# Attention kernel with convolution layout: squared norms from weights times T in PSUM, and a re-ordered head

## The chip, the cores and the metric

The kernel runs on one core of a Trainium2 chip. The metric is the device time of one execution in microseconds (us). TensorE (PE in the profile) multiplies matrices and writes PSUM, VectorE (DVE) and ScalarE (ACT) do elementwise work, GpSimd (POOL) does elementwise work in SBUF, and SyncE (SP) issues the DMAs.

## The reference, cut to what matters

The input x is 16 images of 192 channels by 48 x 48 pixels (n = 2304), float32. Each image is normalised in 32 groups of 6 channels, goes through a channel attention of 8 heads (d = 24), and is added to the input.

```python
xt = _gn(x).reshape(b, c, n).transpose(0, 2, 1)
q, k, v = jnp.split(xt @ w_qkv, 3, axis=-1)        # heads: q, v (b,h,n,d), k (b,h,d,n)
q = q / jnp.maximum(jnp.sqrt(jnp.sum(q * q, axis=-2, keepdims=True)), EPS)
k = k / jnp.maximum(jnp.sqrt(jnp.sum(k * k, axis=-1, keepdims=True)), EPS) * temperature
attn = _softmax(jnp.einsum('bhpn,bhnq->bhpq', k, q))
out = jnp.einsum('bhnp,bhpq->bhnq', v, attn)        # back to (b, n, c)
out = out @ w_out + b_out
return x + out.transpose(0, 2, 1).reshape(b, c, H, W)
```

## The kernel before, in words

**Algebra.** The attention needs only the Gram matrix of the normalised input, G = x x^T (192 x 192 per image). With T = G W the scores are W_q^T T_k, and the squared norms of q and k are the diagonals of W_q^T T_q and W_k^T T_k. The softmax and the two weight matrices fold into one matrix M of 192 x 192 per image, and the output is x + M x_norm + bias. Every float32 factor is split into a high and a low float16 part (names with h and l), and each product is made of three: high x high, low x high, high x low.

**Tiling.** Two images are one pair; there are 8 pairs. A pair lies in three tiles of 128 partitions (t = 0: channels 0 to 127 of the first image, t = 2: of the second, t = 1: channels 128 to 191 of both) by 2304 columns. A *chunk* is one tile by 768 columns; the nine chunks of a pair, CHUNKS[0] to CHUNKS[8], go group by group of columns, in each t = 0, 2, 1. A *slot* is 128 columns of a pair: TensorE transposes its high and low parts into PSUM (`transposes`, L956), ScalarE copies them to SBUF (`to_tok`, L577, a ring of four), and TensorE adds their product to the Gram matrix (`gram`, L981).

**Steps.** The outer loop is step p = -1 to 7. A step has two halves. In the first, A, the 18 slots of pair p+1 run (`transposes` three slots ahead of `gram`), and between them the small work of pair p: `flip`, softmax_in, exp, softmax_out, `attn_values` ("v"), `folded_weights` ("m"). In the second, B, TensorE makes the 18 results of pair p (`result`, five or so products of 384 columns each, into a ring of four PSUM banks, which VectorE empties into x_sb, L855), and between them the small work of pair p+1: `finish_gram`, `gram_weights` ("w0", "w1": T = G W into g_ps banks 0 and 1 for the two images' first 128 channels and s_ps bank 0 for the other 64 of both), "t0" to "t2" (ScalarE takes the high half of T into tq, VectorE the low half), `scores`, `norms`, `spread`. Step -1 has no results, step 7 no slots.

**The order within an engine** is written out by hand: tables PE_A, PE_B, ACT_A, ACT_B, POOL_B, VEC_A, VEC_B say after which slot (A) or result (B) which piece stands, with a FIRST_ set for step -1 and a LAST_ set for step 7's A half and step 6's B half. `hooks` (L335) picks the table. Each engine runs its own list in order and waits on semaphores.

**Splitting a pair.** While pair p's results run, ScalarE normalises the chunks of pair p+2: "x3" writes the float32 value of chunk 3 to the ring xn (three entries, `chunk_value`), "h3" its float16 high part (`chunk_high`), a bare 3 both. GpSimd's `split` subtracts them to get the low part. "x3" waits until GpSimd has read chunk 0 from the ring; "h" of a chunk with t = 0 waits until a third of the last results with that buffer are made. Both need the scale and shift rb, which GpSimd's `group_power` makes from the variance: VectorE's bn_stats ("bn", `piece`) and `channel_stats` ("stats"), TensorE's `group_sums` ("sums"), VectorE's `group_variance` ("var"). Slots 0 to 5 need chunks 0 to 2, slots 6 to 11 chunks 3 to 5, slots 12 to 17 chunks 6 to 8.

**Norms, scores.** `scores` (L1064) makes, for each image and half of the heads, one chain of 6 products of 192 columns (the columns of w_q and w_k beside each other) with the 96 q columns of T as weights, and one chain of 6 products of 96 columns with the k columns: 48 products. VectorE's `norms` multiplies the two diagonal blocks by the identity, sums and clamps them (four instructions, L768 to L771), GpSimd's `norm_power` raises them to -1/2, and `spread` scales the scores. `flip` transposes them for the softmax.

**Head.** Pair 0 is normalised in smaller parts by all three engines (`first_split`, `first_value`, `first_low`, `first_high`). The float16 weights' high parts are made by ScalarE, the low parts by GpSimd (`low_constants`, in SBUF, through xn); TensorE transposes the value weights behind slot 14 (`transpose_wv`), VectorE splits them (`value_weights`). ScalarE's first three values of pair 1 wait for `low_constants`.

Of the kernel before, what the change touches and what calls it, by code (L numbers as in the profile page):

```python
# [101 lines left out]
def preact_attention(nc, x, w_qkv, temperature, w_out, b_out, ident, ident16, groups, headmask, out):  # L102
# [29 lines left out]
    with ExitStack() as ctx:  # L132
# [48 lines left out]
        tq = sb("tq", [P, 3, 2, 2 * C], F16)  # L181
        dg = sb("dg", [HC, 8, HC])
# [33 lines left out]
        qk_ps = s_ps[0:HC, :, 0:2 * C].rearrange("p b (j s c) -> p b j s c", j=2, s=2)  # L216
        kk_ps = g_ps[0:HC, 0, 0:2 * C].rearrange("p (b j c) -> p b j c", b=2, j=2)
# [71 lines left out]
        STAT, GVAR, NORM, DIAG, SOFT, ATTN = 6, 4, 2, 3, 5, 6  # L289
# [231 lines left out]
        def _(act):  # L521
# [729 lines left out]
```

## Time and profile before

| | us |
|---|---|
| median of 3 runs | 374.44 |
| the runs | 373.13, 374.47, 374.44 |
| the profiled execution's own time | 374.76 |
| its span, first to last instruction | 372.8 |
| busy: TensorE / weight loads | 331.2 (89%) / 233.4 (63%) |
| busy: VectorE / ScalarE / GpSimd | 283.2 (76%) / 235.9 (63%) / 150.4 (40%) |
| chain that ended last, shares | PE 64%, ACT 15%, issue 10%, DVE 5%, DMA 2% |

The page divides the span into 40 slices and prints the busy share of each engine and the granted TensorE clock as digits: TensorE is at 9 tenths or more from the eighth slice on but for two near the end, and the clock is below full speed in the sixth to the eighth (47 to 75 us). The rows of the timeline are merged: "x3" is three instructions from the first's start, the time is up to the last's end. Instructions of one engine overlap, so a pitch (start to start) is shorter than a duration. A time in brackets is how long the engine had been idle before, with what ended the wait.

### The profile page before, as it was taken

How to read it: one execution, taken by the hardware profiler on the slowest of the kernel's cores; microseconds unless marked ns; L12 is line 12 of the kernel's file. 1: busy time of each engine (PE TensorE's matmuls, PEld its weight loads, DVE VectorE, ACT ScalarE, POOL GpSimd, SP SyncE). 2: the span in 40 equal slices, each digit the busy share in tenths (PEclk: the TensorE clock that was granted, in tenths of full speed). 3: DMA queues.
4: the chain of work that ended last, by engine and by line, in shares of the span. 5: the costliest groups of instructions: out<-in, count | busy, mean ns of one | idle time of the engine just before them, and what ended most of it. 6: DMA issues, size and time to landing. Idle time of an engine off the chain costs nothing.

```text
span 372.8 us, 9327 instructions
## 1 busy us (share of the span) xinstructions
PE 331.2 (89%) x3724; PEld 233.4 (63%) x3724; DVE 283.2 (76%) x666; ACT 235.9 (63%) x410; POOL 150.4 (40%) x133
## 2 busy tenths in 40 slices
PE   0048856999999999999999999999999999999795
PEld 0036645875778566865777577856686577765452
DVE  4889855887699669986799769966998665359774
ACT  1098489763997299747996399729974699610200
POOL 0079858301970169203950197016920395001000
PEclk9999976899999999999999999999999999999999
DMA  7999900004994279815991499427981563034766
GB/s 235 359 286 246 244 16 3 2 2 139 300 323 132 86 233 326 247 44 137 336 335 44 134 297 338 124 87 226 320 261 45 165 217 88 2 105 150 230 213 192
DMA packets 30826, 67.73 MB, mean 182 GB/s; under 512 B 5504, under 2 KB 12096, under 8 KB 30784
## 3 DMA queue, kind: packets, MB, share of 16 engines
q1 hardware_dynamic: 30544, 66.56, 56.7%
q10 hardware_dynamic: 240, 0.59, 0.6%
q8 instruction: 29, 0.48, 0.5%
q14 instruction: 13, 0.11, 0.1%
HBM read 29.38 MB, written 28.31 MB: 155 GB/s over the span
## 4 chain that ended last, share of the span: by engine, by line
PE 64%; ACT 15%; issue 10%; DVE 5%; DMA 2%; SPq 2%; POOL 1%; ACTq 0%; POOLq 0%
PE u_ps L927 30%; PE g_ps L927 17%; PE s_ps L927 10%; ACT h_sb L543 4%; ACT tok L581 4%; ACT xn L537 3%; PE u_ps L976 2%; DMA wo<-in_L_conv_w_out_dram 2%; PE u_ps L977 2%; ACT h_sb L550 1%; DVE x_sb L855 1%; PE u_ps L979 1%; PE u_ps L978 1%; SPq L354 1%; SPq L359 1%
## 5 line engine op out<-in xcount | busy, mean ns | idle before, releaser
L474 POOL TENSOR_TENSOR l_sb<-xn,h_sb 128x768 f16<-128x768 f32 x63 | 103.8, 1649 | 56.0 <-ACT h_sb L543 55.7
L855 DVE SCALAR_TENSOR_TENSOR x_sb<-u_ps,bias,x_sb 128x384 f32<-128x384 f32 x144 | 85.9, 613 | 24.2 <-PE u_ps L927 24.1
L927 PE MATMUL g_ps<-tok 128*128 128x64 f16 (+1 forms) x864 | 87.1, 241 | 3.4 <-ACT tok L581 2.9
L537 ACT ACTIVATE xn<-x_sb,rb 128x768 f32<-128x768 f32 x63 | 63.6, 1020 | 29.7 <-POOL rb L486 29.7
L581 ACT COPY tok<-u_ps 128x384 f32<-128x384 f32 x144 | 65.0, 485 | 19.8 <-PE u_ps L979 18.6
L927 PEld LDWEIGHTS g_ps<-tok 128*128 128x128 f16 x864 | 57.0, 99 | 28.5 <-ACT tok L581 5.8
L728 DVE BATCH_NORM_STATS2 bnst<-x_sb 128x6 f32<-128x384 f32 x144 | 69.9, 543 | 5.3 <-DMA x_sb<-in_x_dram 5.2
L927 PE MATMUL u_ps<-h_sb,ml 128*128 128x384 f16 (+1 forms) x336 | 73.2, 327 | 0.0
L543 ACT ACTIVATE h_sb<-x_sb,rb 128x768 f16<-128x768 f32 x63 | 64.4, 1022 | 0.0
L976 PE MATMUL u_ps<-id,h_sb 128*128 128x128 f16 x288 | 48.9, 223 | 8.2 <-DVE l_sb L718 7.4
L977 PE MATMUL u_ps<-id,l_sb 128*128 128x128 f16 x288 | 48.9, 223 | 0.0
L927 PE MATMUL u_ps<-h_sb,mh 128*128 128x384 f16 (+1 forms) x192 | 47.2, 326 | 1.5 <-DVE ml L817 1.5
L480 POOL TENSOR_TENSOR grs<-gvar,minus_half 128x3 f32<-128x3 f32 x8 | 7.1, 885 | 102.6 <-DVE gvar L761 102.6
L927 PE MATMUL u_ps<-hl,mh 128*128 128x384 f16 (+1 forms) x192 | 47.9, 334 | 0.0
L927 PE MATMUL u_ps<-l_sb,mh 128*128 128x384 f16 (+1 forms) x192 | 47.1, 326 | 0.0
L927 PEld LDWEIGHTS u_ps<-h_sb,ml 128*128 128x128 f16 (+1 forms) x336 | 28.9, 101 | 23.9 <-issue 7.3
L976 PEld LDWEIGHTS u_ps<-id,h_sb 128*128 128x128 f16 x288 | 27.4, 100 | 8.6 <-ACT h_sb L550 6.5
L978 PE MATMUL u_ps<-id,h_sb 128*128 128x128 f16 x144 | 32.1, 223 | 0.0
L979 PE MATMUL u_ps<-id,l_sb 128*128 128x128 f16 x144 | 32.1, 223 | 0.0
L977 PEld LDWEIGHTS u_ps<-id,l_sb 128*128 128x128 f16 x288 | 28.8, 100 | 0.4
L927 PEld LDWEIGHTS u_ps<-hl,mh 128*128 128x128 f16 (+1 forms) x192 | 14.7, 103 | 15.0 <-issue 7.5
L491 POOL TENSOR_TENSOR r<-n,minus_half 96x8 f32<-96x8 f32 x8 | 13.3, 1660 | 24.9 <-DVE n L771 24.2
(144 smaller groups left out, 567.6 us busy)
## 6 DMA issues: line engine op xcount, KB each, us to landing
x_sb<-in_x_dram SPq DMA_DIRECT2D x48, 384.0 KB, 5.4
out_dram<-x_sb SPq DMA_DIRECT2D x48, 384.0 KB, 2.9
out_dram<-x_sb SPq DMA_DIRECT2D x48, 192.0 KB, 2.8
x_sb<-in_x_dram SPq DMA_DIRECT2D x45, 192.0 KB, 5.4
hl<-h_sb SPq DMA_DIRECT2D x48, 96.0 KB, 2.8
hl<-l_sb SPq DMA_DIRECT2D x48, 96.0 KB, 3.0
x_sb<-in_x_dram ACTq DMA_DIRECT2D x3, 192.0 KB, 4.2
w<-in_L_conv_w_qkv_dram SPq DMA_DIRECT2D x1, 288.0 KB, 7.4
```

The lines of the kernel that those rows point to most:

```text
L474: nc.gpsimd.tensor_tensor(l_sb[:, par, t, cols], xn[:, c % XN_RING, :], h_sb[:, par, t, cols], ALU.subtract).then_inc(l_ok, 1)
L491: nc.gpsimd.tensor_tensor(r8[:, :], n8[:, :], minus_half[0:HC, :].to_broadcast([HC, 8]), ALU.pow).then_inc(r8_ok, 1)
L537: nc.scalar.activation(xn[:, c % XN_RING, :], xcol(q, t, g * GW, GW), ACT.Identity, bias=rb[:, par, 1, t:t + 1], scale=rb[:, par, 0, t:t + ...
L543: nc.scalar.activation(h_sb[:, par, t, g * GW:g * GW + GW], xcol(q, t, g * GW, GW), ACT.Identity, bias=rb[:, par, 1, t:t + 1], scale=rb[:, ...
L581: nc.scalar.copy(tok[:, j % TOK_RING, :, :].rearrange("p b n -> p (b n)").bitcast(F32), slot_words(j)).then_inc(tok_a, 1)
L728: ins = V.bn_stats(bnst[:, t, 6 * part:6 * part + 6], xcol(q, t, part * BW, BW))
L855: V.scalar_tensor_tensor(out=xs, in0=block_ps(n), scalar=bias[:, t:t + 1], in1=xs, op0=ALU.add, op1=ALU.add).then_inc(out_ok, 1)
L927: return nc.tensor.matmul(dst, lhs, rhs, start=start, stop=stop, skip_group_check=True)
L976: nc.tensor.transpose(bank[:, b, 0:P], h_sb[:, par, 2 * b, px], id16[:, :])
L977: nc.tensor.transpose(bank[:, b, 256:384], l_sb[:, par, 2 * b, px], id16[:, :])
L978: nc.tensor.transpose(bank[:, :, P:P + C1], h_sb[:, par, 1, px], id16[:, :])
L979: nc.tensor.transpose(bank[:, :, P + C1:P + 2 * C1], l_sb[:, par, 1, px], id16[:, :]).then_inc(tr_mm, 1)
```

## The change

1. **Norms.** `scores` keeps only the products of q columns of T with w_k: 24 products of 96 columns. After the low half of T is taken (now only the q half, 192 columns), VectorE multiplies T by the weights elementwise, in place in PSUM. ScalarE ("p", `high_products`) and VectorE ("lo", `low_products`) split the product into float16 parts pw16, and TensorE (`squares`) sums it over the partitions: 24 products with 128 columns of pw16 as weights and a 2-column matrix of ones (`side`) as moving operand. `norms` is left with one clamp.
2. **Tables.** Scores stand after result 10 instead of 12, squares after 12. ScalarE makes x0, x1, x2 ahead of t0, "p" between h1 and h2, and x7 moves from ACT_B to slot 1 of ACT_A; there h8 now stands ahead of exp. GpSimd's norms stand ahead of split 4. The last pair has its own places.
3. **Second pair.** In step 0 flip, v and m stand at slots 5, 12 and 15, and ScalarE's pieces h5 to h8 of pair 1 one behind each slot.
4. **Head.** The value weights are transposed and split before pair 0's first split. The group sums of pair 1 stand behind slot 17, ahead of the Gram matrix's end. VectorE makes the low parts wml (`mixed_weights`) and the first three values of pair 1 (`second_value`), ahead of z.

```diff
-PE_B = {0: ["gram"], 2: ["sums"], 4: ["w0"], 6: ["w1"], 12: ["scores"]}
-ACT_A = {0: ["h6"], 2: ["h7"], 4: ["x8"], 6: ["exp", "h8"], 11: ["v"], 14: ["m"]}
-ACT_B = ["x0", "t0", "t1", "t2", "h0", 1, 2, 3, 4, 5, "x6", "x7"]
-POOL_B = ["power", 0, 1, 2, 3, 4, "norms", 5, 6, 7, 8]
+PE_B = {0: ["gram"], 2: ["sums"], 4: ["w0"], 6: ["w1"], 10: ["scores"], 12: ["squares"]}
+ACT_A = {0: ["h6"], 1: ["x7"], 2: ["h7"], 3: ["x8"], 5: ["h8"], 6: ["exp"], 11: ["v"], 14: ["m"]}
+ACT_B = ["x0", "x1", "x2", "t0", "t1", "t2", "h0", "h1", "p", "h2", 3, 4, 5, "x6"]
+POOL_B = ["power", 0, 1, 2, 3, "norms", 4, 5, 6, 7, 8]
-VEC_B = {0: ["gram"], 2: ["var"], 4: ["z"], 6: ["t0", "t1", "t2"], 12: ["norms"], 17: ["spread", "bn", "bn", "bn", "bn"]}
+VEC_B = {0: ["gram"], 2: ["var"], 4: ["z"], 6: ["t0", "t1", "t2"], 9: ["lo"], 12: ["norms"], 17: ["spread", "bn", "bn", "bn", "bn"]}
-FIRST_PE_A = {14: ["wv"]}
-FIRST_PE_B = {0: ["gram", "sums"], 2: ["w0"], 7: ["w1", "scores"]}
+FIRST_PE_A = {17: ["sums"]}
+FIRST_PE_B = {0: ["gram"], 2: ["w0"], 7: ["w1", "scores", "squares"]}
-FIRST_ACT_B = [0, "x1", "t0", "t1", "t2", "h1", 2, 3, 4, 5, "x6", "x7"]
-FIRST_POOL_B = ["power", 0, 1, 2, 3, 4, "norms", 5, 6, 7, 8]
-FIRST_VEC_A = {17: ["bn"] * 7 + ["stats", "wv"]}
-FIRST_VEC_B = {0: ["gram", "var", "z", "t0", "t1"], 1: ["t2", "bn", "bn", "wo", "norms", "spread", "bn", "bn"]}
+FIRST_ACT_B = ["h0", "h1", "h2", "x3", "t0", "t1", "t2", "h3", "p", "x4", "h4", "x5"]
+FIRST_POOL_B = ["power", 0, 1, 2, 3, 4, 5, "norms", 6, 7, 8]
+FIRST_VEC_A = {17: ["bn"] * 7 + ["stats"]}
+FIRST_VEC_B = {0: ["var", "gram", "wm", "v0", "v1", "v2", "z", "t0", "t1"],
+               1: ["t2", "lo", "bn", "bn", "norms", "wo", "spread", "bn", "bn"]}
+SECOND_PE_A = {5: ["flip"], 12: ["v"], 15: ["m"]}
+SECOND_ACT_A = {0: ["h5"], 1: ["x6"], 2: ["h6"], 3: ["x7"], 4: ["h7"], 5: ["x8"], 6: ["h8"], 8: ["exp"], 14: ["v"], 17: ["m"]}
-LAST_PE_B = {0: ["gram"], 2: ["w0"], 3: ["w1"], 5: ["scores"], 10: ["flip"], 16: ["v"]}
+LAST_PE_B = {0: ["gram"], 2: ["w0"], 3: ["w1"], 6: ["scores"], 7: ["squares"], 11: ["flip"], 16: ["v"]}
-LAST_ACT_B = ["t0", "t1", "t2", "exp", "v"]
+LAST_ACT_B = ["t0", "t1", "t2", "p", "exp", "v"]
-LAST_VEC_B = {0: ["gram"], 2: ["z"], 3: ["t0", "t1", "t2"], 5: ["norms"], 8: ["spread"], 10: ["soft_in"], 12: ["soft_out"],
-              15: ["v"]}
+LAST_VEC_B = {0: ["gram"], 2: ["z"], 3: ["t0", "t1", "t2"], 4: ["lo"], 6: ["norms"], 9: ["spread"], 11: ["soft_in"], 13: ["soft_out"], 15: ["v"]}
...
-                if q == 1 and c < XN_RING:
-
-                    act.wait_ge(low_ok, 8)
...
-                nc.scalar.copy(tq[:, k, 0, :], src[:, 0:2 * C]).then_inc(th_ok, 1)
+                nc.scalar.copy(tq[:, k, 0, :], src[:, 0:C]).then_inc(th_ok, 1)
+
+            def high_products(q):
+
+                need(act, n_mm, q)
+                for k in range(3):
+                    act.wait_ge(pw_ok, 3 * q + k + 1)
+                    nc.scalar.copy(pw16[:, k, 0, 0:2 * C], t_ps(k)).then_inc(ph_ok, 1)
...
+            def mixed_weights():
+
+                dve.wait_ge(high_ok, 1)
+                for b in (0, 1):
+                    r = slice(C1 * b, C1 * b + C1)
+                    V.scalar_tensor_tensor(out=wml[r, b, :], in0=w1[r, qk], scalar=W_SCALE, in1=wmh[r, b, :],
+                                           op0=ALU.mult, op1=ALU.subtract).then_inc(wm_ok, 1)
...
+            def second_value(c):
+
+                t, g = CHUNKS[c]
+                if c == 0:
+
+                    dve.wait_ge(norm, 2 * NORM)
+                    dve.wait_ge(low_ok, 4)
+                V.tensor_scalar(xn[:, c, :], xcol(1, t, g * GW, GW), rb[:, 1, 0, t:t + 1], rb[:, 1, 1, t:t + 1],
+                                ALU.mult, ALU.add).then_inc(xn1_vec, 1)
...
             def norms(q):
 
+                dve.wait_ge(n_mm, q + 1)
+                V.tensor_scalar(n8[:, :], n_ps[0:HC, :], NORM_EPS ** 2 * NORM_FACTOR, None, ALU.max).then_inc(diag, 1)
...
-                V.tensor_tensor(tq[:, k, 1, :], src[:, 0:2 * C], tq[:, k, 0, :], ALU.subtract).then_inc(tl_ok, 1)
+                V.tensor_tensor(tq[:, k, 1, :], src[:, 0:C], tq[:, k, 0, :], ALU.subtract).then_inc(tl_ok, 1)
+                dve.wait_ge(tl_ok, 3 * q + k + 1)
+                V.scalar_tensor_tensor(out=src[:, 0:2 * C], in0=src[:, 0:2 * C], scalar=W_SCALE, in1=(w1 if k == 2 else w0)[:, 0:2 * C],
+                                       op0=ALU.mult, op1=ALU.mult).then_inc(pw_ok, 1)
+
+            def low_products(q):
+                for k in range(3):
+
+                    dve.wait_ge(ph_ok, 3 * q + k + 1)
+                    V.tensor_tensor(pw16[:, k, 1, 0:2 * C], t_ps(k), pw16[:, k, 0, 0:2 * C], ALU.subtract).then_inc(pl_ok, 1)
...
+                        terms = [(tq[:, b, 0, qc], wh0[:, kc]), (tq[:, b, 1, qc], wh0[:, kc]), (tq[:, b, 0, qc], wl0[:, kc]),
+                                 (tq[:, 2, 0, qc], wmh[:, b, kc]), (tq[:, 2, 1, qc], wmh[:, b, kc]),
+                                 (tq[:, 2, 0, qc], wml[:, b, kc])]
+                        for k, (lhs, w) in enumerate(terms):
+                            last = mm(qk_ps[:, b, j, :], lhs, w, k == 0, k == 5)
                 last.then_inc(s_mm, 1)
+
+            def squares(q):
+
+                pe.wait_ge(pl_ok, 3 * q + 3)
+                for a in range(4):
+                    c = C - C * (a // 2) + HC * (a % 2)
+                    terms = [(pw16[:, k, i, c:c + P], side[:, k, :]) for k in range(3) for i in (0, 1)]
+                    dst = n_ps.rearrange("p (s b j) -> p s j b", s=2, b=2)[:, a // 2, a % 2, :]
+                    for k, (lhs, one) in enumerate(terms):
+                        last = mm(dst, lhs, one, k == 0, k == len(terms) - 1)
+                last.then_inc(n_mm, 1)
```

## Rows read from the trace of the kernel before

**Rows 1.** Windows: stretch, length; busy PE, PEld, DVE, ACT, POOL; clock, DMA share, GB/s

```profile
79.80:120.25 40.45, 40.37 (x467) 28.31 (x466) 32.87 (x80) 29.91 (x51) 17.96 (x14) 1.00 0.63 206
```

**Rows 2.** Timeline of TensorE in one pair: start, us, instructions, [idle before]

```profile
124.68 0.32 PE L927 MATMUL u_ps<-parts,grp 128*128 128x6 bf16 x7
124.86 0.32 PE L927 MATMUL u_ps<-h_sb,mh 128*128 128x384 f16 x1
...
136.74 0.33 PE L927 MATMUL s_ps<-wh,tq 128*96 128x192 f16 x2
...
137.23 0.25 PE L927 MATMUL g_ps<-wh,tq 128*96 128x96 f16 x2
...
137.50 0.33 PE L927 MATMUL s_ps<-wh,tq 128*96 128x192 f16 x2
...
139.79 0.33 PE L927 MATMUL u_ps<-h_sb,mh 128*128 128x384 f16 x1
...
153.16 0.25 PE L927 MATMUL s_ps<-wvh,ax 96*96 96x192 f16 x1
```

**Rows 3.** Timeline of ScalarE in the same pair

```profile
127.91 1.03 ACT L537 ACTIVATE xn<-x_sb,rb 128x768 f32<-128x768 f32 x1 [4.43 <-POOL rb L486]
130.96 0.86 ACT L626 CAST tq<-g_ps 128x384 f16<-128x384 f32 x2 [2.02 <-PE g_ps L927]
...
142.23 1.94 ACT L537 ACTIVATE xn<-x_sb,rb 128x768 f32<-128x768 f32 x2
144.62 0.48 ACT L581 COPY tok<-u_ps 128x384 f32<-128x384 f32 x1 [0.46 <-PE u_ps L979]
...
149.98 0.26 ACT L587 ACTIVATE s_ps<-s_ps 96x96 f32<-96x96 f32 x1
...
151.06 1.24 ACT L581 COPY tok<-u_ps 128x384 f32<-128x384 f32 x3
```

**Rows 4.** Timeline of VectorE in the same pair

```profile
131.47 1.02 DVE L848 TENSOR_TENSOR tq<-g_ps,tq 128x384 f16<-128x384 f32 x2 [0.22 <-ACT tq L626]
...
150.27 0.25 DVE L799 TENSOR_REDUCE sm<-s_ps 96x4 f32<-96x96 f32 x1
...
151.06 0.56 DVE L805 TENSOR_TENSOR s_ps<-s_ps,mask 96x384 f32<-96x384 f32 x1
...
152.25 0.55 DVE L808 TENSOR_TENSOR ax<-s_ps,ax 96x384 f16<-96x384 f32 x1
```

**Rows 5.** Timeline of GpSimd in the same pair

```profile
151.26 1.65 POOL L474 TENSOR_TENSOR l_sb<-xn,h_sb 128x768 f16<-128x768 f32 x1 [1.83 <-ACT h_sb L543]
```

**Rows 6.** Chain of work that ended last: start, us, what

```profile
72.21 0.06 PE u_ps L976
...
81.12 0.81 PE u_ps L927 x5
```

**Rows 7.** Timeline of TensorE in the head

```profile
43.90 0.32 PE L927 MATMUL s_ps<-parts,grp 128*128 128x6 bf16 x7
...
80.96 0.33 PE L927 MATMUL u_ps<-h_sb,mh 128*128 128x384 f16 x1
```

**Rows 8.** Timeline of ScalarE in the head

```profile
47.57 1.03 ACT L537 ACTIVATE xn<-x_sb,rb 128x768 f32<-128x768 f32 x1 [3.10 <-POOL rb L486]
...
61.56 0.47 ACT L581 COPY tok<-u_ps 128x384 f32<-128x384 f32 x1
```

**Rows 9.** Timeline of VectorE in the head

```profile
41.69 0.77 DVE L746 CAST parts<-res 128x6 bf16<-128x6 f32 x1
...
53.16 3.23 DVE L689 SCALAR_TENSOR_TENSOR wol<-wo,woh 96x384 f16<-96x384 f32 x2
```

**Rows 10.** Timelines of ScalarE, GpSimd and TensorE for the last pair

```profile
330.08 0.86 ACT L626 CAST tq<-g_ps 128x384 f16<-128x384 f32 x2 [4.37 <-PE g_ps L927]
...
338.15 1.64 POOL L491 TENSOR_TENSOR r<-n,minus_half 96x8 f32<-96x8 f32 x1 [23.46 <-DVE n L771]
...
349.66 0.26 PE L927 MATMUL s_ps<-woh,vh 96*128 96x192 f16 x1 [0.28 <-DVE vl L814]
```

More of the change, by code:

```diff
@@ L180, in preact_attention @@
         z16 = sb("z16", [P, 2, C], F16)
-        tq = sb("tq", [P, 3, 2, 2 * C], F16)
-        dg = sb("dg", [HC, 8, HC])
+        tq = sb("tq", [P, 3, 2, C], F16)
+        pw16 = sb("pw16", [P, 3, 2, 2 * C + P - HC], F16)
+        side = sb("side", [P, 3, 2], F16)
         n8 = sb("n8", [HC, 8])
@@ L270, in preact_attention @@
         r8_ok = sem("r8_ok")
+        pw_ok = sem("pw_ok")
+        ph_ok = sem("ph_ok")
+        pl_ok = sem("pl_ok")
+        n_mm = sem("n_mm")
         diag = sem("diag")
@@ L322, in for_pairs, with hooks @@
                 step(p)
-        def hooks(p, first, usual, last, last_step):
-            at_end = isinstance(p, int) and p == last_step
-            return first if isinstance(p, int) and p < 0 else last if at_end else usual
+        def hooks(p, first, usual, last, last_step, second=None):
+            if p == 0 and second:
+                return second
+            return first if p < 0 else last if p == last_step else usual
         block = ctx.enter_context(nc.Block())
@@ L472, in split @@
                     pool.wait_ge(h_ok, (q - 1) * NC_ + c + 1)
-                    pool.wait_ge(xn_ok, (q - 1) * NC_ + c + 1)
+                    if q == 1 and c < XN_RING:
+                        pool.wait_ge(xn1_vec, c + 1)
+                    else:
+                        pool.wait_ge(xn_ok, (q - 1) * NC_ + c + 1 - XN_RING)
                     nc.gpsimd.tensor_tensor(l_sb[:, par, t, cols], xn[:, c % XN_RING, :], h_sb[:, par, t, cols],
@@ L542, in chunk_high @@
                 t, g = CHUNKS[c]
+                if q == 1 and c == 0:
+                    act.wait_ge(norm, 2 * NORM)
                 nc.scalar.activation(h_sb[:, par, t, g * GW:g * GW + GW], xcol(q, t, g * GW, GW), ACT.Identity,
@@ L647, in step @@
                         to_tok(p + 1, j)
-                    for what in hooks(p, FIRST_ACT_A, ACT_A, LAST_ACT_A, PAIRS - 1).get(j, ()):
+                    for what in hooks(p, FIRST_ACT_A, ACT_A, LAST_ACT_A, PAIRS - 1, SECOND_ACT_A).get(j, ()):
                         if first:
@@ L673, in _ @@
             V.memset(wl1[C1:P, :], 0.0)
+            V.memset(pw16[:, :, :, 2 * C:], 0.0)
+            ones = ((0, slice(0, P), 0), (1, slice(0, P), 1), (2, slice(0, C1), 0), (2, slice(C1, P), 1))
+            for k, rows, b in ones:
+                V.memset(side[rows, k, b:b + 1], 1.0)
+                V.memset(side[rows, k, 1 - b:2 - b], 0.0)
             for z in (wmh, wml):
@@ L858, in _ @@
             small_steps = {"gram": low_gram, "z": z_copy, "t0": lambda q: low_t(q, 0), "t1": lambda q: low_t(q, 1),
-                           "t2": lambda q: low_t(q, 2), "norms": norms, "spread": spread, "soft_in": softmax_in,
+                           "t2": lambda q: low_t(q, 2), "lo": low_products, "norms": norms, "spread": spread, "soft_in": softmax_in,
                            "soft_out": softmax_out, "v": low_v, "m0": low_m0, "m1": low_m1}
@@ L899, in step @@
                             pieces(now, 1)
-                        elif what == "wv":
-                            value_weights()
                         elif small:
@@ L916, in step @@
                             out_weights()
+                        elif what == "wm":
+                            mixed_weights()
+                        elif what in ("v0", "v1", "v2"):
+                            second_value(int(what[1]))
                         elif gram:
@@ L962, in transposes @@
                     in_tok(q, j - RING)
+                if q == 0 and j == RING - 1:
+                    pe.wait_ge(wv_ok, 2)
                 if q == 0 and j * P % BW == 0:
@@ L1166, in _ @@
             small_steps = {"gram": finish_gram, "w0": lambda q: gram_weights(q, False),
-                           "w1": lambda q: gram_weights(q, True), "scores": scores, "flip": flip,
+                           "w1": lambda q: gram_weights(q, True), "scores": scores, "squares": squares, "flip": flip,
                            "v": attn_values, "m": folded_weights}
@@ L1186, in step @@
                             transposes(p + 1, 1 - par, j + AHEAD)
-                    for what in hooks(p, FIRST_PE_A, PE_A, LAST_PE_A, PAIRS - 1).get(j, ()):
+                    for what in hooks(p, FIRST_PE_A, PE_A, LAST_PE_A, PAIRS - 1, SECOND_PE_A).get(j, ()):
                         if what == "sums":
@@ L1190, in step @@
                                 group_sums(p + 2, first)
-                        elif what == "wv":
-                            transpose_wv()
                         elif small:
```

54 lines of the change are left out of this document (21 added, 33 removed).

## The prediction

> **What bounds the kernel now.** I read the windows by stage first: who is busy where. Over one pair of images (79.80 to 120.25 us) TensorE is busy 40.37 of 40.45 us, VectorE 32.87, ScalarE 29.91, GpSimd 17.96 [rows 1]. The timeline repeats itself after each such window, so there are three stages: a head to the first result at 80.96 [rows 7], six equal periods of 40.45 us and a tail from 80.96 + 6 x 40.45 = 323.7, where the last pair's small products and its results follow each other. A busy TensorE row is not yet a full one, since matmuls overlap, so I read the timeline of each engine through one period.
>
> A period has two halves. In half B (results n = 0 to 17 of a pair, with the next pair's small products between them) TensorE issues without a gap: it ends last. In half A (18 slots: transposes, ScalarE's copy into tok, gram) that is not so. ScalarE's copy tok0 starts at 144.62, having waited for the transposes, and from there ScalarE runs without a pause: copies at a pitch of 0.37 us, chunk pieces (x = value, h = high part) at 0.92 us, exp at 149.98, tok7 at 151.06 [rows 3]. Seven copies and three pieces are 7 x 0.37 + 3 x 0.92 = 5.35 us, which is 149.98 - 144.62. TensorE's gram 7 waits for tok7, and attn_values ("v") starts at 153.16, 2.10 us after tok7 [rows 2, 3]. So **from tok0 to v (8.54 us) ScalarE sets the pace**, not TensorE; from v to the next tok0 TensorE does.
>
> **Steady periods: what TensorE saves.** Scores take 139.79 - 136.74 = 3.05 us; a group of six products of 96 columns takes 137.50 - 137.23 = 0.27 us, 0.045 each, and the products of 192 columns take the rest [rows 2]. The change leaves 24 products of 96 columns: 24 x 0.045 = 1.08 us. It adds "squares": 24 products with 2 moving columns, each with 128 columns of weights. Nearest row: the seven group sums (6 moving columns, 128 of weights) start at 124.68 and the next product at 124.86, 0.026 each [rows 2]. Upper bound: the transposes with their own 128 columns of weights, 0.06 each in the chain [rows 6] (0.056 by their starts). I take 0.026, as the form is nearly the same: 0.62 us, and 0.12 us by my allowance for the first load. Half B gets shorter by 3.05 - 1.08 - 0.62 - 0.12 = **1.23 us** (0.5 at the upper bound). The Trainium skill, "TensorE: Matmul & The Clock Gate", section "Back-to-back issue gap", gives 81 ns per product for a stream of loads and products at 128 columns; by that page squares would be an estimated 1.9 us and the saving nothing. The trace's 0.056 us for that very form speaks against it.
>
> Does half B keep up? On VectorE t0 to t2 become a half-wide subtraction (0.36 us; two full ones take 1.02), a handover of 0.03 and a product in place in PSUM (0.56, the row with PSUM in and out, 0.61 at most) [rows 4]: three take 2.85 us instead of 1.5. From 131.3 (t0 on ScalarE at 130.96, now half as wide) the last product stands at 134.1, results 7 to 9 at 135.8, "lo" (3 x 0.47) at 137.3. A result takes TensorE 0.81 us at least [rows 6], up to 0.95; scores, now two results earlier (135.0 to 136.1), and results 11 and 12 behind them put squares at 137.8: 0.5 us of cover. "p" on ScalarE (three copies, 1.14 us) waits for the last product until about 134.5; behind it are queued h2 to x6. ScalarE had waited 4.43 us for the norm at 127.91 and 2.02 us for t0 at 130.96 [rows 3]; x1 and x2 now fill the second wait, x7 leaves half B, so even with p it is free at about 142.8, before the transposes let tok0 start (144.62 - 1.23 = 143.39). On GpSimd the power of the norms stands behind split 3 instead of 4 and ends near 141.6; spread wants it at 143.7. The removed diagonal work of VectorE (four instructions, some 2 us) was beside TensorE's work: nothing on the path.
>
> **What half A gives back.** ACT_A now has h6, x7, h7, x8, h8 ahead of exp, where it had h6, h7, x8. From tok0 to exp: 7 x 0.37 + 5 x 0.92 = 7.19 us instead of 5.35. VectorE's softmax_out starts 0.29 us after exp does and runs from 150.27 to 152.80, 2.53 us [rows 3, 4]; TensorE's v waits for it, 0.06 us more. v comes at 7.19 + 0.29 + 2.53 + 0.06 = 10.07 us after tok0. The other way to v, over tok7, gives 7.19 + 0.17 (exp) + 2.10 = 9.46. So softmax_out is late next, with TensorE idle. Queued behind v are the slots 8 to 17, folded_weights and the next results; they follow at their old distance, since vl and ml had more slack than this. Balance of a period: 10.07 - 8.54 - 1.23 = **+0.30 us**; six: +1.8 us (+1.4 to +6 with the bounds). TensorE does less and the period gets no shorter.
>
> **The head.** Before, the sums of pair 1 stand behind the gram's end (43.90) [rows 7], statistics having been slowed by GpSimd's low parts of the weights (a cast of six elements took 0.77 us) [rows 9]. With the two low parts on VectorE instead, and the sums first, they start at about 42.7; seven small steps on VectorE and three on GpSimd bring the norm to about 46.0, where ScalarE's wait ended at 47.57 [rows 8]. The value weights move before the first split: TensorE has nothing there, VectorE loses some 0.9 us by them, which the four weight transposes taken out of the slots' end give back to TensorE (about as long). VectorE then does the mixed weights, v0 to v2 and only then z. No row has a VectorE pass of 768 columns from SBUF to SBUF; bounds are half of ScalarE's 0.92 and GpSimd's 1.65; I take 0.94, twice VectorE's pitch for 384 columns (1.02 - 0.55 = 0.47 [rows 4]), and 0.5 each for the two weights of 384. z is then read at 48.9 (47.16 before), but ScalarE has four pieces ahead of t0 (46.0 to 49.7) and hardly waits. Then: t0 at 49.8, the last subtraction at 52.4, 24 products at half clock (1.2 GHz, as there now) to 54.5, squares to 55.3, tok0 at 56.3 behind x5, where it was 61.56 [rows 8]. But seven pieces now stand between the first seven slots, 1.29 us each: tok7 at 65.3, v (slot 12) at 70.7, vl at 73.1, m at 73.7, then on VectorE six statistics, m0, two, m1: 78.1. The results wait for m1 and start at 78.2, where they started at 80.96 [rows 7]: TensorE idles some 1.9 us ahead of them. **Head: -2.8 us** of the 5.3 that tok0 gains.
>
> **The tail.** t0 of the last pair starts at 330.08 [rows 10]; the three products stand at 333.3, result 4 and lo follow to 335.4, squares run to 336.2, and after one small step the power can start at 336.65, where it stood at 338.15 [rows 10]. Flip now stands behind result 11 instead of 10, so the softmax follows only 1.0 us earlier; one result fewer lies between softmax_out and vl, and m (349.66 before [rows 10]) comes at 348.5. From m on nothing changes. **Tail: -1.15 us.**
>
> **Sum.** -2.8 + 1.8 - 1.15 = -2.15 us on the profiled execution's own 374.76 us (span 372.8 and 1.96 around it): 372.6. That run is 0.3 above the median of 374.44; I forecast **372.4**.
>
> **Rivals.**
> 1. *Softmax is not last*: v follows tok7. For it: only 0.61 us between the two ways; against it: each term is a row. Six times -0.61: 368.7.
> 2. *TensorE's saving counts in full*: only if ScalarE isn't the pace from tok0 on, which rows 3 contradict. 6 x 1.53 less: 363.2.
> 3. *The head's gain is lost*: VectorE's weights and passes wait for GpSimd. For it: the cast of 0.77 us, and 3.23 us for two instructions on wol while GpSimd works [rows 9]. Two and three such passes at 1.65 us put z at 45.1 + 8.25 = 53.3 and, less ScalarE's 0.9 of cover, all after it 3.5 us later: 375.9. The Trainium skill, "SBUF — State Buffer", section "Who interferes with whom", names copy, cast and tensor_scalar, and any instruction with two SBUF inputs, as those that VectorE shares a port for; both kinds are added here.
> 4. *Slower: squares cost 0.056 us each* [rows 6]: 0.72 us more in each of six periods, and 1.2 us in head and tail: 377.9. It decides from about 0.047 us each on.
> 5. *Slower: the reciprocal waits for GpSimd*. GpSimd's last split takes 1.65 us and started at 151.26, 1.28 us after exp [rows 3, 5]. With h8 ahead of exp it starts 0.2 us before exp and covers softmax_out's second instruction, the reciprocal, 0.6 us after exp. No row shows that form beside GpSimd; for waiting speaks the cast of rows 9, against it only that a reciprocal is another operation. It would be held 0.9 us, six times: 377.8.
>
> **How the numbers follow.** Forecast 0.44 (its own range 370.4 to 374.4), rival 1 0.14, rival 2 0.06, rival 3 0.13, rival 4 0.13, rival 5 0.10. A measurement of this kernel tells about 0.5% (1.87 us) from no change: faster is below 372.57. Half of the forecast's chance (0.23), rivals 1 and 2 and little more: 0.45 faster; the rest of it with most of rival 3: 0.31 same; rivals 4 and 5: 0.24 slower. The range takes in rivals 1, 3, 4 and 5, leaving out rival 2: 368.2 to 378.2.
>
> **What would show it.** In the timeline after: scores 1.1 us and squares 0.7 us; exp 7.2 us after tok0 and v 10.1 after it, with TensorE waiting for ax; a period of 40.75 us; tok0 of pair 1 near 56.3 and the first result at 78.2 with a wait for ml ahead; ScalarE waiting for TensorE ahead of each steady tok0. If v follows tok7 at once, or tok0 waits for x6, the balance of the period is wrong; a period under 40.2 us ends the forecast.

## The result and the profile after

| | before | after |
|---|---|---|
| median | 374.05 us (5 runs, 373.13 to 374.47) | 376.44 us (5 runs, 376.40 to 378.86) |
| the profiled execution: own time, span | 374.76, 372.8 us | 378.86, 377.1 us |
| busy TensorE / VectorE / ScalarE / GpSimd | 331.2 / 283.2 / 235.9 / 150.4 us | 328.8 / 290.2 / 240.3 / 145.8 us |
| chain that ended last | PE 64%, ACT 15%, DVE 5% | PE 53%, ACT 22%, DVE 14% |

The ratio is 1.0096 (95% interval 1.0072 to 1.0121): the kernel became **slower by about 1%** (the medians lie 0.6% apart), where I forecast 372.4 us. The time lies in my range and on the wrong side. The profiled execution is the longest of the five: four ran at a mean granted clock of 0.985 and this one at 0.972. In its profile two stretches of the last pair's products run at half clock; the other four were not profiled.

The windows of two pairs, in the columns of [rows 1]:

```profile
118.88:160.14 41.26, 39.74 (x466) 26.89 (x465) 33.53 (x83) 30.85 (x54) 17.75 (x14) 1.00 0.62 202
160.14:201.41 41.27, 39.75 (x468) 26.90 (x466) 33.53 (x83) 30.84 (x54) 17.74 (x14) 1.00 0.62 202
```

TensorE has 0.6 us less to do than in [rows 1] and the period is 0.82 us longer: its idle time went from 0.08 to 1.5 us. ScalarE's timeline of that pair, from its first piece x0 to v (the columns of [rows 3]):

```profile
167.80 2.86 ACT L551 ACTIVATE xn<-x_sb,rb 128x768 f32<-128x768 f32 x3 [4.43 <-POOL rb L503]
...
174.79 1.05 ACT L560 ACTIVATE h_sb<-x_sb,rb 128x768 f16<-128x768 f32 x1
177.35 1.03 ACT L551 ACTIVATE xn<-x_sb,rb 128x768 f32<-128x768 f32 x1 [1.51 <-PE u_ps L982]
...
182.88 1.01 ACT L551 ACTIVATE xn<-x_sb,rb 128x768 f32<-128x768 f32 x1
183.80 0.45 ACT L598 COPY tok<-u_ps 128x384 f32<-128x384 f32 x1
...
190.98 0.24 ACT L604 ACTIVATE s_ps<-s_ps 96x96 f32<-96x96 f32 x1
```

The row at 177.35 is x3, with 1.51 us of idle time ahead of it, ended by TensorE's result. From there to tok0 at 183.80 no row has a wait: seven pieces stand back to back, and tok0 has lost the 0.46 us that it waited for the transposes in [rows 3]. **ScalarE now sets tok0.** TensorE in the same pair, with scores, squares and v:

```profile
174.99 0.29 PE L982 MATMUL s_ps<-wh,tq 128*96 128x96 f16 x2
...
176.20 0.35 PE L982 MATMUL u_ps<-hl,mh 128*64 128x384 f16 x2
...
177.96 0.74 PE L982 MATMUL s_ps<-side,pw 128*128 128x2 f16 x24
...
193.84 0.28 PE L982 MATMUL s_ps<-wvh,ax 96*96 96x192 f16 x1 [0.19 <-DVE ax L851]
```

I cut each period into three: from ScalarE's x0 (the end of its wait for the norm) to tok0, from tok0 to v, and from v to the next x0. That is 16.71, 8.54 and 15.20 us before [rows 1 to 3] (the last is the period less the other two), and 16.00, 10.04 and 15.23 after. The same cut is used for every kernel below.

### The profile page after: what moved, and what is told of

The parts are those of the page before. It is cut to its first block, busy times and chain, and to the rows that moved or that the text cites. A ratio compares the mean times of both kernels' runs of the same rounds, so it can differ in the third digit from the quotient of the medians.

```text
span 377.1 us, 9396 instructions
## 1 busy us (share of the span) xinstructions
PE 328.8 (87%) x3724; PEld 222.6 (59%) x3724; DVE 290.2 (77%) x704; ACT 240.3 (64%) x431; POOL 145.8 (39%) x129
## 4 chain that ended last, share of the span: by engine, by line
PE 53%; ACT 22%; DVE 14%; issue 6%; DMA 2%; SPq 2%; POOL 0%; ACTq 0%; POOLq 0%
PE u_ps L982 25%; PE g_ps L982 13%; PE s_ps L982 10%; ACT h_sb L560 9%; ACT xn L551 7%; ACT tok L598 5%; DVE bnst L775 3%; DMA wo<-in_L_conv_w_out_dram 2%; PE u_ps L1033 2%; PE u_ps L1034 1%; DVE s_ps L848 1%; DVE ax L850 1%; DVE ax L851 1%; DVE xn L765 1%; SPq L370 1%
## 5 line engine op out<-in xcount | busy, mean ns | idle before, releaser
L907 DVE SCALAR_TENSOR_TENSOR x_sb<-u_ps,bias,x_sb 128x384 f32<-128x384 f32 x144 | 87.1, 615 | 30.4 <-PE u_ps L982 30.2
L551 ACT ACTIVATE xn<-x_sb,rb 128x768 f32<-128x768 f32 x60 | 60.2, 1023 | 36.0 <-POOL rb L503 27.0
L982 PEld LDWEIGHTS g_ps<-tok 128*128 128x128 f16 x864 | 56.2, 99 | 36.7 <-ACT tok L598 15.6
L598 ACT COPY tok<-u_ps 128x384 f32<-128x384 f32 x144 | 66.2, 477 | 16.4 <-PE u_ps L1036 14.6
L982 PE MATMUL u_ps<-h_sb,ml 128*128 128x384 f16 (+1 forms) x336 | 74.4, 331 | 0.0
```

What stands on the lines that cost most here:

```text
L551: nc.scalar.activation(xn[:, c % XN_RING, :], xcol(q, t, g * GW, GW), ACT.Identity, bias=rb[:, par, 1, t:t + 1], scale=rb[:, par, 0, t:t + ...
L598: nc.scalar.copy(tok[:, j % TOK_RING, :, :].rearrange("p b n -> p (b n)").bitcast(F32), slot_words(j)).then_inc(tok_a, 1)
L907: V.scalar_tensor_tensor(out=xs, in0=block_ps(n), scalar=bias[:, t:t + 1], in1=xs, op0=ALU.add, op1=ALU.add).then_inc(out_ok, 1)
L982: return nc.tensor.matmul(dst, lhs, rhs, start=start, stop=stop, skip_group_check=True)
```

## The experiments

In each, the tables of the kernel after are edited unless said otherwise. Cuts are of the pair near 165 to 209 us of the profiled execution, in us; ratios are to the kernel before, timed on the same chip, and not all rows were timed on one chip. In five kernels the periods differ from pair to pair; the mean of five is 40.58 us in e5, 39.94 in e7, 40.88 in e12, 39.59 in e11 and 39.70 in e13.

| kernel | x0 to tok0 | tok0 to v | v to x0 | period | ratio (95%) |
|---|---|---|---|---|---|
| before | 16.71 | 8.54 | 15.20 | 40.45 | 1 |
| after | 16.00 | 10.04 | 15.23 | 41.27 | 1.0096 (1.0072 to 1.0121) |
| e1_x3_first | 15.59 | 10.06 | 15.22 | 40.87 | 1.0035 (1.0009 to 1.0060) |
| e6_scores_at_11 | 15.34 | 10.05 | 15.23 | 40.62 | 1.0005 (0.9973 to 1.0037) |
| e4_squares_twice | 16.19 | 10.06 | 15.23 | 41.48 | 1.0140 (1.0093 to 1.0187) |
| e2_exp_first | 16.01 | 9.57 | 15.19 | 40.77 | 1.0000 (0.9969 to 1.0031) |
| e5_h8_behind_tok7 | 15.59 | 9.60 | 15.73 | 40.92 | 0.9933 (0.9909 to 0.9958) |
| e8_filler | 16.00 | 10.05 | 15.22 | 41.27 | 1.0073 (1.0056 to 1.0090) |
| e9_sums_behind_gram | 16.00 | 10.05 | 15.23 | 41.27 | 1.0153 (1.0126 to 1.0179) |
| e7_spread | 16.29 | 8.27 | 15.30 | 39.86 | 0.9860 (0.9826 to 0.9895) |
| e10_before_order | 16.72 | 8.29 | 15.19 | 40.20 | 0.9948 (0.9925 to 0.9970) |
| e12_loads_earlier | 16.31 | 8.27 | 16.51 | 41.09 | 0.9980 (0.9947 to 1.0013) |
| e11_spread_filler | 16.09 | 8.27 | 15.19 | 39.55 | 0.9856 (0.9817 to 0.9895) |
| e13_norms_behind_4 | 15.55 | 8.30 | 16.09 | 39.94 | 0.9811 (0.9775 to 0.9847) |

**What holds tok0.** `split` puts the wait for the results ahead of a plain `3`, thus ahead of x3 and h3 both, though only h3 writes where the results still read. First, x3 alone is taken out from behind it:

```
-ACT_B = [..., "p", "h2", 3, 4, 5, "x6"]
+ACT_B = [..., "p", "h2", "x3", "h3", 4, 5, "x6"]
```

> One table entry changed in the kernel after: ScalarE's piece 3 is taken apart, so that the value x3 stands ahead of the wait for result 11 and only the high part h3 behind it. Theory A (this wait, ahead of x3 instead of h3, makes ScalarE late for tok0): x3 runs at about 175.8 instead of 177.35 in the trace's terms, the idle 1.51 us shrinks to about 0.6, tok0 then waits for the transposes, which TensorE has issued by 183.2, and starts 0.43 us earlier. Period 41.27 - 0.43 = 40.84 us, time 376.4 - 6 x 0.43 = 373.9. Rival B (tok0 isn't held by ScalarE's queue but the period is set elsewhere, by TensorE in half B or by the transfers): period and time unchanged, 41.27 and 376.4.

Measured: 40.87 us. ScalarE's timeline of that kernel shows x3 running early, a wait of 0.60 us left to h3, and TensorE last again ahead of tok0:

```profile
176.13 1.03 ACT L551 ACTIVATE xn<-x_sb,rb 128x768 f32<-128x768 f32 x1
177.76 1.03 ACT L560 ACTIVATE h_sb<-x_sb,rb 128x768 f16<-128x768 f32 x1 [0.60 <-PE u_ps L982]
...
183.80 0.48 ACT L598 COPY tok<-u_ps 128x384 f32<-128x384 f32 x1 [0.41 <-PE u_ps L1036]
```

Then the other end of the same wait, by one number: `PE_B = {..., 11: ["scores"], ...}` instead of 10.

> One number changed in the kernel after: TensorE's scores stand behind result 11 instead of result 10, so result 11, for which ScalarE waits ahead of x3, is not held up by them. Theory A (the wait ahead of x3 is what makes ScalarE late for tok0): result 11 is complete 1.2 us earlier, the idle ahead of x3 falls from 1.51 to about 0.3 us, tok0 waits for the transposes again and the period is as with x3 moved, 40.85 us against 41.27; ratio to before about 1.0035. Rival B (x3 moved gained by something else, such as an earlier x4): period stays at 41.27.

```profile
173.53 1.03 ACT L551 ACTIVATE xn<-x_sb,rb 128x768 f32<-128x768 f32 x1 [0.18 <-PE u_ps L982]
...
180.65 0.48 ACT L598 COPY tok<-u_ps 128x384 f32<-128x384 f32 x1 [0.57 <-PE u_ps L1036]
```

The wait shrank to 0.18 us and the period to 40.62, 0.23 us better than expected and 0.25 better than e1. TensorE's timelines say why. In e1 (as in the kernel after) scores stand between results 10 and 11, in e6 behind both:

```profile
174.63 0.35 PE L982 MATMUL u_ps<-hl,mh 128*64 128x384 f16 x2
...
175.40 0.29 PE L982 MATMUL s_ps<-wh,tq 128*96 128x96 f16 x2
...
176.61 0.35 PE L982 MATMUL u_ps<-hl,mh 128*64 128x384 f16 x2
...
177.56 0.33 PE L982 MATMUL u_ps<-h_sb,mh 128*128 128x384 f16 x1
```

```profile
171.73 0.35 PE L982 MATMUL u_ps<-hl,mh 128*64 128x384 f16 x2
172.41 0.33 PE L982 MATMUL u_ps<-hl,mh 128*64 128x384 f16 x2
173.33 0.25 PE L982 MATMUL s_ps<-wh,tq 128*96 128x96 f16 x2
...
174.41 0.33 PE L982 MATMUL u_ps<-h_sb,mh 128*128 128x384 f16 x1
```

From result 10 to result 12 it is 2.93 us in e1 and 2.68 in e6, with the same products. Results 10 and 11 are a pair of products on 64 columns each; pulled apart, they cost 0.25 us more. In e6 half B is 16.71 - 15.34 = 1.37 us shorter than before, which is 3.05 - 1.08 - 0.60: the whole of TensorE's saving.

**What squares cost.** In e1 all 24 are issued twice in six periods (`for a in 2 * [0, 1, 2, 3] if 1 <= q <= 6 else range(4)`).

> The kernel with x3 ahead of the wait (e1_x3_first), and in it the 24 products of squares are issued twice in each of the six steady periods. Theory A (with the wait out of the way TensorE sets the start of tok0, and squares cost what their starts show, 0.60 us): period 40.84 + 0.60 = 41.44 minus ScalarE's idle left, at least 41.3; time 376.5 to 377.5. Theory A' (ScalarE is still last ahead of tok0, by the wait that h3 keeps): a small part of 0.6 only, period about 40.9. Rival B (24 products with weights of their own cost 0.056 us each, 1.3 us): period 42.2, time 382.

```profile
177.64 1.34 PE L982 MATMUL s_ps<-side,pw 128*128 128x2 f16 x48
```

The period is 0.61 us over e1's: 24 products cost 0.60 us, 0.025 each, on the path. Rival 4 is out. My 1.9 us for squares by the Trainium skill, "TensorE: Matmul & The Clock Gate", section "Back-to-back issue gap", took its figure for products that move 128 columns; squares move 2, so the figure says nothing of them.

**What holds v.** exp is put ahead of h8: `6: ["exp", "h8"]` instead of `5: ["h8"], 6: ["exp"]`.

> One table entry changed in the kernel after: exp stands ahead of h8 (both at slot 6), where h8 stood at slot 5 ahead of it. Theory A (softmax_out on VectorE, started by exp, lets v start): exp comes 0.92 us earlier, softmax_out then ends 9.15 us after tok0 and the way over tok7 (9.46 us after tok0) is last, so v starts 0.58 us earlier and the period is 40.69, time 376.4 - 3.5 = 372.9. Rival B (v follows tok7 already): no change, 376.4. Rival C (TensorE's own work from tok0 to v is as long): no change either, and no wait ahead of v in either kernel.

Measured: v 9.57 us after tok0 instead of 10.04, without a wait for ax. Softmax_out was last, by 0.47 us; the trace of e5 shows what comes next, TensorE's slots. A stronger form, on top of e1, has `5: ["exp"], 7: ["h8"]`:

> The kernel with x3 ahead of the wait (e1_x3_first), and in it exp at slot 5 and h8 at slot 7, behind tok7. Theory A: exp at 6 x 0.37 + 4 x 0.92 = 5.9 us after tok0, softmax_out ends at 8.78, tok7 at 6.44 and v from it at 8.54; v 8.78 us after tok0 instead of 10.04, period 40.84 - 1.26 = 39.6, time 373.9 - 7.6 = 366.3. Rival B (the steady period's loss isn't in ScalarE's order, but in TensorE's slots): under 0.3 us per period over e1_x3_first, time above 372. Rival C (h8 is then late for the low part l8 on GpSimd, which the transposes of slot 12 want): TensorE waits for l_sb ahead of the transposes of slot 12, and most of the 1.26 us comes back there; 372 or more.

v came at 9.60, not 8.78. TensorE's timeline of that kernel:

```profile
185.07 0.61 PE L982 MATMUL g_ps<-tok 128*128 128x384 f16 x6 [0.34 <-ACT tok L598]
186.37 0.61 PE L982 MATMUL g_ps<-tok 128*128 128x384 f16 x6 [0.34 <-ACT tok L598]
...
188.71 0.60 PE L982 MATMUL g_ps<-tok 128*128 128x384 f16 x6
189.49 0.60 PE L982 MATMUL g_ps<-tok 128*128 128x384 f16 x6
190.26 0.25 PE L982 MATMUL s_ps<-wvh,ax 96*96 96x192 f16 x1
```

While a piece stands between every two copies, slots come every 1.29 us and TensorE idles 0.34 us in each (ahead of grams 2, 3 and 4); from gram 4 (186.37) they come every 0.78 us back to back, and v stands behind five of them. That time can't be won by exp. Theory A failed, and neither rival is as written: B has the right place, TensorE's slots, but it is ScalarE's pieces that hold them up. Hence e7, with one piece fewer in half A, and of h6, h7 and x8 no two in neighbouring slots: h6, h7, x8 behind tok0, tok2, tok4, exp behind tok5, h8 behind tok7, x7 back in half B, scores at 11 and x3 apart:

```
+PE_B = {0: ["gram"], 2: ["sums"], 4: ["w0"], 6: ["w1"], 11: ["scores"], 12: ["squares"]}
+ACT_A = {0: ["h6"], 2: ["h7"], 4: ["x8"], 5: ["exp"], 7: ["h8"], 11: ["v"], 14: ["m"]}
+ACT_B = [..., "p", "h2", "x3", "h3", 4, 5, "x6", "x7"]
```

> Tables alone changed against the kernel after: scores behind result 11, x3 apart from h3 and x7 back in half B, and in half A h6, h7, x8 behind tok0, tok2, tok4, exp behind tok5 and h8 behind tok7, so that pieces never follow in neighbouring slots. Theory A (ScalarE's order takes what TensorE saves): TensorE has no wait in half A beyond the copy's 0.3 us at its start; v 8.0 to 8.5 us after tok0 against 10.04, tok0 set by the transposes, period 41.27 - 0.4 - 1.6 = 39.3 us if nothing else is last. Rival B (the loads of x become last, for which VectorE's statistics waited up to 0.9 us in the run with h8 behind tok7): the period stays near 40.3 and VectorE waits for the input's transfer ahead of its statistics and m1 in most periods. Rival C (x7 no longer fits half B): tok0 follows x7 with no wait for the transposes, period about 39.8.

v comes 8.27 us after tok0, and behind the first gram TensorE has no wait on the way. The number of pieces ahead of exp (four, now three) and their places changed together, and no run has four pieces spread out. The mean period is 39.94 us, not 39.3. Rivals B and C both take a part, by these rows of VectorE and ScalarE (the pair ahead of the one in the table, and that one):

```profile
151.82 1.02 DVE L775 BATCH_NORM_STATS2 bnst<-x_sb 128x6 f32<-128x384 f32 x2 [0.69 <-DMA x_sb<-in_x_dram]
154.06 1.02 DVE L775 BATCH_NORM_STATS2 bnst<-x_sb 128x6 f32<-128x384 f32 x2 [1.22 <-DMA x_sb<-in_x_dram]
```

```profile
179.44 1.03 ACT L551 ACTIVATE xn<-x_sb,rb 128x768 f32<-128x768 f32 x1 [0.66 <-POOL l_sb L491]
180.37 0.46 ACT L598 COPY tok<-u_ps 128x384 f32<-128x384 f32 x1
```

Statistics wait for the loads of x, and x7 for GpSimd's l4, so tok0 follows x7. The kernel is 1.4% faster than before. Is that the order alone? The kernel BEFORE with the same exp and h8 answers:

> The kernel BEFORE with one table entry changed: in half A exp behind tok5 and h8 behind tok7, where both stood behind tok6. This asks how much of the 1.4% that the reordered kernel (e7_spread) gains is open to the old small products as well. Theory A (the change of the small products is worth something, once ScalarE's order lets it through): here v can come no earlier than TensorE's own slots allow, 8.0 to 8.5 us after tok0 against 8.54, so the period stays within 40.0 to 40.45 and the time is 0 to 0.7% under before, well above e7_spread's 0.986. Rival B (the order alone does it): ratio to before 0.99 or lower, period under 40.0.

0.9948: 0.25 us of its period came from the order, and v comes 8.29 us after tok0, TensorE's pace. The rest, 0.9% (0.9860 to 0.9948), came with the new kernel, its small products and its head together. The profiles put more of it in the head: of 3.3 us of span (369.08 and 365.82), 1.9 lie ahead of the first result (78.77 and 76.88), and the mean periods differ by 0.26 us. Two more runs took the two new waits one by one. Loads earlier in SP's queue (`LOAD_LAG = 1`):

> The reordered kernel (e7_spread) with LOAD_LAG 1 instead of 2: each load of x is queued on SP one chunk earlier, behind the landing of the store before. Theory A (the loads are what is last in e7_spread's steady periods, where VectorE's statistics waited up to 1.22 us for them): the waits for the transfer ahead of the statistics disappear and the period falls from 39.94 on average to about 39.4, time 3 us lower. Rival B (SP's queue now stands still for a store's landing of about 4.3 us with later stores, copies and loads behind it): the loads end no earlier, period the same or longer, up to 1 us per period. Rival C (the loads hide, and the period is set by GpSimd's low parts, for which x7 waits 0.66 us): waits for the transfer go but the period stays within 0.1 us.

Rival B: v to x0 grew to 16.51 us, and over the steady stretch the statistics waited 10.4 us for the transfer, 5.2 in e7. The last load of that pair landed 32.5 us behind x0, 30.6 in e7. Loads that land later lengthen the period; that they set every period of e7 isn't shown. And the power of the norms behind l4 (`POOL_B = ["power", 0, 1, 2, 3, 4, "norms", 5, ...]`), on e11 below:

> The reordered kernel with doubled results (e11_spread_filler), and on GpSimd the power of the norms behind the low part l4 instead of l3, as in the kernel before. There x7 waited 0.66 us for l4 and tok0 followed x7. Theory A (ScalarE's chain to x7 sets tok0): x7 no longer waits, tok0 starts 0.66 us earlier, period 39.55 - 0.66 = 38.9 us where the loads of x allow it, time about 3 us under e11_spread_filler's, ratio 0.978. Rival B (the power now ends 1.65 us later and spread, then flip, wait for it): tok0 earlier but v no earlier, period 39.5 or more. Rival C (the loads are last): the period stays at 39.5 and VectorE's waits for the transfer ahead of the statistics grow by what tok0 gains.

tok0 came 0.54 us earlier (15.55), x7 without a wait, and v to x0 took 16.09 instead of 15.19 us, with waits of 0.85 and 0.55 us for the loads. One of five periods was 39.08, the mean 39.70, where e11 has 39.59: rival C for the most part. Its time is the best measured, **1.9% under before**; its interval overlaps those of e7 and e11, it was timed on another chip, and as its mean period is no shorter than e11's, the profiles don't show a gain from the move.

**The tail.** The granted clock falls to half (1.2 GHz) in some executions behind TensorE's wait ahead of the last v. In e8 results 15 and 16 of the last pair but one are issued twice, which overwrites itself and fills that wait (`for again in range(2 if q == PAIRS - 2 and n in (15, 16) else 1):`).

> The kernel after, in which TensorE issues the products of results 15 and 16 of the last but one pair twice (1.6 us of work that overwrites itself) in the 1.86 us that it waits ahead of v of the last pair. Theory A (that wait is what lets the granted clock fall in the tail, in those executions where it falls): time 376.4 in nearly all executions, granted clock 0.985 or higher, no stretch at half clock behind v, the last chain entry of TensorE at 15.5 us. Rival B (the fall has nothing to do with this wait): executions still lie between 376.4 and 378.9, and the clock falls in the tail in some. If the doubled results stand on the path: all executions up to 1.6 us longer.

The timeline of TensorE in the tail of the kernel after, then its windows, then a window of e8:

```profile
348.66 0.28 PE L982 MATMUL s_ps<-wvh,ax 96*96 96x192 f16 x1 [1.86 <-DVE ax L851]
...
355.62 0.32 PE L982 MATMUL u_ps<-h_sb,mh 128*128 128x384 f16 x1 [1.54 <-DVE ml L860]
```

```profile
348.66:352.60 3.94, 3.94 (x25) 2.61 (x26) 3.02 (x6) 0.95 (x2) 0.00 (x0) 0.57 0.59 220
352.60:355.70 3.10, 1.55 (x23) 1.21 (x21) 1.50 (x4) 1.84 (x5) 0.00 (x0) 0.99 0.53 135
355.70:359.70 4.00, 4.00 (x15) 1.98 (x15) 1.24 (x2) 0.00 (x0) 0.00 (x0) 0.57 0.35 96
```

```profile
348.77:352.70 3.93, 3.81 (x45) 2.86 (x45) 3.10 (x6) 1.33 (x3) 0.00 (x0) 1.00 0.69 244
```

In e8 v has no wait and the full clock; from v to the first result of the last pair it is about 5.7 us (354.45 - 348.77) against 6.96. The last chain entry is 15.48 us, 17.16 in the kernel after. Its six executions took 374.7 to 376.0 us, ratio 1.0073 (1.0056 to 1.0090). That interval overlaps the one of the kernel after, so the profiles carry this reading more than the times. Nine profiles have a wait of 1.85 or 1.86 us ahead of v. Windows of 1.5 us behind v show half clock there in five (after, e4, e7, e9, e12) and not in four (e1, e2, e5, e6); in the kernel before and e10 (0.96 us of wait) and in e8, e11 and e13 (results doubled) there is none. Four of the nine had none either, so three profiles with the filler fit the reading, that the wait lets the clock fall, without proving it.

The filler on top of e7:

> The reordered kernel (e7_spread) with results 15 and 16 of the last but one pair issued twice in TensorE's wait ahead of the last v. Theory A (the clock falls behind that wait in some executions, and only there and behind the wait for ml): the profile shows the full clock behind v, the way from v to the first last-pair result is 5.7 us instead of 6.95, and the median is about 1 us under e7_spread's, near 366.5, ratio 0.983. Rival B: a stretch at half clock follows v here too, and the time is that of e7_spread.

The profile shows the full clock behind v and 5.66 us from v to the first result (e7: 6.95). The median ratio, 0.9856, isn't to be told from e7's.

**The head.** One part of it is undone, the sums of pair 1 behind the gram's end (`FIRST_PE_B = {0: ["gram", "sums"], ...}`).

> One part of the new head undone in the kernel after: the sums of pair 1 stand behind the gram's end again, as before. Theory A (the head's gain comes through the norm of pair 1): the sums start at about 43.7 us instead of 42.1, ScalarE's h0 at 47.2 instead of 45.7, tok0 of pair 1 at about 58.0 instead of 56.5 and the first result at 79.6 instead of 78.1; time +1.5 us over the kernel after, ratio to before 1.0135. Rival B (the first result is set by something that doesn't hang on the norm): first result unchanged at 78.1, time unchanged.

The sums start at 43.66 instead of 42.09, h0 at 46.86 instead of 45.67, tok0 at 57.18 instead of 56.54 and the first result at 78.71 instead of 78.10. By these two profiles the sums alone are worth 0.6 us, not 1.5: half of the delay disappears in ScalarE's waits ahead of t0 to t2. The size is rough. In the eleven kernels with the same head the first result comes at 76.88 (e7) to 79.30 us (e1), which takes in e9's 78.71. Most of that spread arises ahead of pair 0's tok0 (24.27 to 26.26): counted from there, the first result follows after 52.45 to 53.05 us in the eleven, after 53.50 in e9 and 56.34 in the kernel before. And e9's ratio, 1.0153, is 0.57% or 2.1 us above that of the kernel after, near the 1.0135 expected; its four executions ran at a mean clock of 0.975 to 0.979, so a part of that can be half clock in the tail, as in its trace. Between 0.6 and 1.5 us the times don't decide. The other parts of the head weren't undone.

## Why the prediction was wrong, point by point

- **Head: right, to the digit by luck.** TensorE's first result, VectorE and ScalarE in the kernel after:

```profile
78.10 0.34 PE L982 MATMUL u_ps<-h_sb,mh 128*128 128x384 f16 x1 [1.37 <-DVE ml L860]
```

```profile
45.67 3.19 DVE L765 TENSOR_SCALAR xn<-x_sb,rb 128x768 f32<-128x768 f32 x3
48.78 0.35 DVE L885 COPY z<-s_ps 128x384 f16<-128x384 f16 x1
```

```profile
56.54 0.48 ACT L598 COPY tok<-u_ps 128x384 f32<-128x384 f32 x1
```

  Predicted 78.2, 48.9 and 56.3. Against [rows 7] the head gives 2.86 us (2.8 said). Both are single executions, and other kernels with this head lie from 1.2 us ahead of 78.10 to 1.2 behind; counted from pair 0's tok0 the gain is 3.3 to 3.9 us. A pass of 768 columns took 1.06 us by its share of the three (0.94 taken), and the two weights of 384 columns 1.13 us (1.0 taken), both beside GpSimd's work. Rival 3 is out: GpSimd didn't hold them up.
- **Softmax behind five pieces: right.** exp 7.18 us after tok0 (7.19), v 10.04 (10.07). Rival 1 is out, and the reciprocal took 0.17 us beside GpSimd's last split, so rival 5 is out.
- **Pace from tok0 to v: right, but narrowly.** With the order changed alone (e10) v came 8.29 us after tok0 instead of 8.54: TensorE's own slots allow 8.29, so ScalarE's pace cost 0.25 us.
- **TensorE's half B: the step that failed.** I wrote "so even with p it is free at about 142.8, before the transposes let tok0 start". I had let x3 run ahead of the wait for results, and had read that wait against the old place of result 11; the change itself moves scores ahead of result 11, 1.2 us later. The row with 1.51 us shows it, and e1 and e6 confirm it from both ends of the wait. Half B got 0.71 us shorter, not 1.23. The 0.52 between them: 0.41 for ScalarE (e1), 0.25 for results 10 and 11 pulled apart (e6 against e1), less the 0.14 by which squares were cheaper than I allowed (0.60 against 0.74). Period: 0.30 + 0.52 = 0.82 us, as measured. My own sign for this case, "tok0 waits for x6", is what the profile shows.
- **The size of the period's loss** is then 6 x 0.82 = 4.9 us, where I had 1.8.
- **Tail: half right.** The power starts at 339.06, 1.8 us earlier against the last steady period's end than in [rows 10] (1.5 predicted). v has its wait of 1.86 us (0.96 before), which I foresaw as the later flip but did not price: the clock. Behind it the results before m and m itself run at half clock, so of the 1.15 us to m some 0.4 are left (1.35 in e8, with the full clock), and the last results take 17.16 us instead of 15.48.
- **The sum**, by the two profiled executions. To the first result: -2.86 us. From there to v of the last pair but one (314.95, now 317.64): +5.55, of which the six periods are 4.9; 0.45 more lies between the first result and the first x0, 0.2 in the first period (41.49). From that v to the last pair's m: -0.39. From m to the last pair's first result: +0.34. From there to the end: +1.66. Together +4.30 us, 372.8 to 377.1. I had -2.15. Of the 6.45 us between, 3.1 are the periods, 0.65 the stretch before them and the first one, and 2.8 the tail, nearly all of it clock: e8, with the full clock behind v and behind the wait for ml, has a span of 374.2 us. The other four executions have 374.6 to 375.7.
- **What hit by luck.** The measured time lies in the range because that took in rivals 1, 3, 4 and 5, and none of these is what happened.

## What to carry to other kernels

When a step is moved ahead of another one, list who waits for the completion of the one that is now later, and read in the code what stands behind that wait, instruction by instruction; here 0.4 us per period hung on whether a wait stood ahead of x3 or of h3. Where two engines feed each other slot by slot, try side work in every second slot: with four pieces in neighbouring slots v came 9.60 us after tok0, with three in every second slot 8.27 (how much of that is the place and how much the fourth piece wasn't taken apart). And before an order is blamed or praised, give the same order to the old kernel, as e10 did.

## What the hardware showed that I had not expected

- A product with 2 moving columns and its own 128 columns of weights took 0.025 us in a row of 24, half of a transpose's 0.056 us with as many weight columns.
- Two products on 64 columns each that stand next to another such pair cost 0.25 us less than with 96-column products in between (2.68 against 2.93 us for the same work).
- The granted clock of TensorE fell to half for some 3 us behind a wait of 1.85 us in five profiles out of nine, and behind the wait of 1.54 us for ml in four (after, e5, e6, e9) of the fourteen that all have it; behind 0.96 us or less ahead of v it fell in none. It costs 1.3 us at the first place (6.96 against 5.67 us from v to the next result) and 1.7 at the second (17.16 against 15.48). Why it falls in one execution and not in the next, no run here shows.
- SP's loads of x were hidden before (VectorE's statistics waited 0.3 us for them over all steady periods) and became last in some periods near 40 us: 5.2 us of waits in e7, where one period of 40.51 us followed waits of 0.69 and 1.22, and eleven waits of up to 1.12 us in e13. In e11 waits of up to 0.57 us left v to x0 at 15.2 us.
